# Preparing six of eight tiles inside the scan steps, and outer products written to PSUM in pairs of words

## The reference, cut to what matters

```
xn    = layernorm(x)
bc    = xn @ W_bc.T                          # 64 + 32 + 32 columns
delta = softplus(bc[..., :64] @ W_dt.T + b_dt)
B, C  = bc[..., 64:96], bc[..., 96:128]
h     = exp(delta * A) * h + (delta * xn) * B      # for each step of time, channel, state
y     = sum over the states of h * C  +  xn * D_param
x     = x + y
```

## Time and profile before

| | |
|---|---|
| median of three runs | 1005.86 us |
| profiled execution, its own time | 1001.59 us |
| its span, first to last instruction | 999.9 us |
| first scan starts | 222.79 us |
| last scan ends | 812.71 us |
| PE busy | 873.0 us, 87% |
| DVE busy | 831.2 us, 83% |
| ACT busy | 460.2 us, 46% |
| POOL busy | 395.3 us, 40% |
| DMA engines busy, mean | 38.1% of the span |
| mean granted TensorE clock | 0.903 |

### The profile page before, as it was taken

The page is one execution under the profiler, slowest core; times in us unless marked ns, Lnnn a source line. Parts: engine busy times, 40 slices in busy tenths (PEclk is TensorE's granted clock), DMA queues, the critical chain, the costliest instruction groups (busy, mean ns, idle before and its releaser), DMA issues.

```text
span 999.9 us, 22490 instructions
## 1 busy us (share of the span) xinstructions
PE 873.0 (87%) x7440; PEld 670.1 (67%) x7440; DVE 831.2 (83%) x861; ACT 460.2 (46%) x798; POOL 395.3 (40%) x737
## 2 busy tenths in 40 slices
PE   5666666159999999999999999999999969899994
PEld 3434444148777777777777777777777747787873
DVE  6655765307999999999999999999999976899884
ACT  1554444533454545544545545454545334443631
POOL 6253333412333333333333333333333544456434
PEclk9776555556999999999999999999999989999997
DMA  9399999392222222222222221222222334210101
GB/s 329 84 150 162 165 170 171 88 163 82 64 65 78 61 76 67 59 77 66 61 79 63 68 72 61 76 64 61 79 64 64 110 106 138 56 51 22 43 22 63
DMA packets 206072, 89.93 MB, mean 90 GB/s; under 512 B 139220, under 2 KB 191956, under 8 KB 205268
## 3 DMA queue, kind: packets, MB, share of 16 engines
q1 hardware_dynamic: 206036, 89.49, 38.1%
HBM read 45.85 MB, written 43.61 MB: 89 GB/s over the span
## 4 chain that ended last, share of the span: by engine, by line
PE 65%; SPq 16%; DVE 8%; POOL 4%; issue 3%; ACT 2%; DMA 1%; ACTq 0%; DVEq 0%; POOLq 0%
PE psum L1329 23%; PE psum L1298 13%; PE psum L1286 11%; PE psum L1336 9%; SPq L974 7%; SPq L1027 6%; PE psum L458 5%; POOL arena L399 2%; DVE arena L1606 2%; SPq L991 1%; POOL arena L390 1%; SPq L968 1%; PE psum L527 1%; DVE delta_mov L706 1%; ACT arena L564 1%
## 5 line engine op out<-in xcount | busy, mean ns | idle before, releaser
L1606 DVE TENSOR_TENSOR_SCAN arena<-arena,psum 128x1024 f32<-128x1024 f32 x256 | 570.9, 2274 | 48.4 <-DMA delta_terms<-arena 29.4
L1429 ACT ACTIVATE arena<-psum 128x512 f32<-128x512 f32 x512 | 278.0, 595 | 303.4 <-PE psum L1286 299.7
L1329 PEld LDWEIGHTS psum<-du_mov,b_sta 96*128 96x128 bf16 x2048 | 206.8, 131 | 130.2 <-DVE arena L1606 127.2
L1329 PE MATMUL psum<-du_mov,b_sta 96*128 96x128 bf16 x2048 | 273.0, 315 | 13.2 <-DVE arena L1606 13.1
L1180 POOL TENSOR_TENSOR carry<-arena 128x64 f32<-128x64 f32 x252 | 110.7, 439 | 357.0 <-DVE arena L1606 270.4
L1286 PE MATMUL psum<-delta_mov,a_sta 96*128 96x128 bf16 x2048 | 163.5, 224 | 8.3 <-ACT arena L1429 8.3
L1286 PEld LDWEIGHTS psum<-delta_mov,a_sta 96*128 96x128 bf16 x2048 | 144.1, 110 | 11.2 <-ACT arena L1429 10.7
L1336 PE MATMUL psum<-carry,ident 128*128 128x32 f32 x1024 | 149.2, 270 | 0.0
L1336 PEld LDWEIGHTS psum<-carry,ident 128*128 128x128 f32 x1024 | 148.4, 206 | 0.0
L1298 PE MATMUL psum<-arena,c_sta 128*32 128x512 f32 x1024 | 148.0, 643 | 0.0
L458 PE MATMUL psum<-delta_mov,arena 128*128 128x256 f32 (+6 forms) x544 | 114.6, 368 | 8.0 <-ACT arena L579 7.9
(11 more groups left out here) (142 smaller groups left out, 819.7 us busy)
## 6 DMA issues: line engine op xcount, KB each, us to landing
du_terms<-arena SPq DMA_DIRECT2D x48, 256.0 KB, 3.9
du_mov<-du_terms SPq DMA_DIRECT2D x128, 96.0 KB
y<-y_rows SPq DMA_DIRECT2D x32, 256.0 KB
b_terms<-delta_mov SPq DMA_DIRECT2D x6, 1024.0 KB, 10.6
delta_terms<-arena SPq DMA_DIRECT2D x48, 128.0 KB, 5.3
delta_mov<-delta_terms SPq DMA_DIRECT2D x128, 48.0 KB
b_sta<-b_terms SPq DMA_DIRECT2D x64, 96.0 KB
arena<-in_L_attn_x SPq DMA_DIRECT2D x8, 512.0 KB, 5.3
```

Source lines behind the costliest of these rows:

```text
L1329: mm = nc.tensor.matmul(sub(psum, 0, P, o, (4, 4), (TS, GD // 2)), b_sta[k][0:ROWS, (s * 4 + tg) * P:(s * 4 + tg + 1) * P], sub(du_mov[k], ...
L1429: nc.scalar.activation(sub(arena, 0, P, k * CHUNK_ELEMS + u * 16 * TS, (TS, 16), (D * TS, SUBS), (1, TS)), sub(psum, 0, P, (4 + u % 2) * B ...
L1606: nc.vector.tensor_tensor_scan(state[s][:, seg], decay[k][:, (s * D + g * GD) * TS:(s * D + (g + 1) * GD) * TS], psum[:, 2 * (step % 2) * ...
```

## The change

*Preparation.* Only tiles 0 and 1 are prepared ahead of the scans. Tiles 2 to 7 are prepared within the 32 scan steps of a tile, two tiles ahead: while tile lt is scanned, tile lt + 2 is prepared (EARLY = 2). Each engine's list gets pieces (`p_piece`) behind the work of a step, by the number n of the step in the tile, 0 to 31:

- SP: x at the tile's start, behind a wait for all stores of the tile before; base in the second chunk, b in the third, delta and du in the fourth, the delta stores ahead of the y store, the du stores behind it, and the loads for the chunk after the next behind that.
- VectorE: statistics at 2 and the shift -mean * rstd at 4, nothing else.
- ACT: the normalisation at 5 (four activations of 256), copies of transposes at 6 and 7, Abs and Relu of the pre-activation at 11 and 15, Exp and the copies of c and b at 16, b at 17 and 18 with Ln at 18, delta's high part at 22, du at 23 and 24 with delta's middle part, du's high part at 26 and middle part at 28 (two casts of 1024 each).
- POOL: rstd at 3, base at 6 and 8, b's parts at 18 and 19, delta at 20, du at 21, delta's rest at 23 and low part at 25, du's rest at 27 and low part at 29.
- TensorE: transposes of xn at 6 and 7, the products for delta one a step at 8 to 15, c and b at 16, transposes of b at 17 and of du at 23 and 24.

Delta is now made with channels on the partitions, from xn transposed and one product of the two weights, W_dt W_bc (`w_eff`), made once. It needs no transpose; du does.

*Buffers.* The decay of a chunk's first half has one buffer in place of two, so the exponentials of the next chunk start two steps later and wait group by group for the scan (AHEAD = 2). y has one row buffer and one bank in place of two. Bank 7 is used for the preparation.

*Outer products.* The scratch rows of du hold, for each channel, a zero word-half and the value (512 bf16 in place of 256), in three parts and not six terms. The operand is loaded so that two time steps stand interleaved, the first row block with its value in the even place and the second in the odd one. A matmul still has 96 rows and 128 columns, and its output is pairs of adjacent words, two pairs at a distance of 8, in place of single words at a distance of 4. The loads for a chunk are 12 DMAs of du, 4 of b and 12 of delta. The delta scratch is laid out by tile, so that parts and batches have one stride.

*Zero fill.* The fill of the b scratch is issued by ACT, in three DMAs, and no longer by SP in six.

The core of the diff:

```
-                            for half in range(2):
-                                for tg in (1, 2, 3, 0):
-                                    o = (pair_bank + half) * BANK + tg
-                                        sub(psum, 0, P, o, (4, 4), (TS, GD // 2)),
-                                        sub(du_mov[k], 0, ROWS, (s * 4 + tg) * D + d0, (DU_COLS, 4), (1, GD // 2)),
+                                    o = (pair_bank + half) * BANK + 4 * tg
+                                        sub(psum, 0, P, o, (2, 2), (TS, GD // 2), (1, 2)),
+                                        sub(du_mov[k], 0, ROWS, (s * 4 + tg) * DU_ROW + 2 * d0, (DU_SIDE, 2), (1, GD)),

 # SP, within the scans
+            def m_tile(lt, first, stream, last):
+                p = lt + EARLY
+                if stream:
+                    sp_.wait_ge(terms_stored[0], 16 * STORES * (p - 1))
+                    load_x(p, 0)
+                for kk in range(CT):
+                    c, k = CT * lt + kk, kk % 2
+                    if not (last and kk >= 2):
+                        sp_.wait_ge(S["args_ready"], (c + 1) * UNITS)
+                        ...
+                        load_md(lt + (kk + 2) // CT, (kk + 2) % CT)
+                    if stream and kk == 1:
+                        store_base(p, 0)
+                    if stream and kk == 3:
+                        sp_.wait_ge(S["dlo_ready"], p)
+                        store_delta(p, 0)
+                    if not (first and kk == 0):
+                        store_y(c - 1)
+                    if stream and kk == 2:
+                        store_b(p, 0)
+                    if stream and kk == 3:
+                        sp_.wait_ge(S["ulo_ready"], p)
+                        store_du(p, 0)
+                    if not (last and kk >= 2):
+                        sp_.wait_ge(S["b_ready"], (c + 1) * STEPS)
+                        load_mu(c + 2, k)

 # POOL, behind the carry and the reset of step n
+            def p_piece(p, n, first):
+                if n == 3:
+                    rstds(p, 0)
+                if n == 6:
+                    pool.wait_ge(S["xn_ready"], p - 1)
+                    base_product(p, 0, sp[0])
+                if n == 8:
+                    base_sum(p, 0, sp[0])
+                ...
+                if n == 20:
+                    delta_sum(p, 0)
+                if n == 21:
+                    du_product(p, 0)
+                if n == 23:
+                    delta_rest(p, 0)
+                if n == 25:
+                    delta_low(p, 0)
+                if n == 27:
+                    du_rest(p, 0)
+                if n == 29:
+                    du_low(p, 0)

 # VectorE, behind the scan of step n
+            def p_piece(p, n, first):
+                if n == 2:
+                    dve.wait_ge(x_loaded[0], 16 * p)
+                    statistics(p, 0)
+                if n == 4:
+                    dve.wait_ge(S["rstd_ready"], p + 1)
+                    nc.vector.scalar_tensor_tensor(out=shift, in0=mv[0][:, 0:7:2], scalar=-1.0, in1=rstd[0], ...)

 # ACT, behind the exponentials of step n
+                if n == 18:
+                    b_middle(p, 0)
+                    ln_part(p, 0)
+                if n == 22:
+                    act.wait_ge(base_stored[0], 16 * p)
+                    delta_high(p, 0)
+                if n == 24:
+                    take_du(p, 0, 1, 7)
+                    delta_middle(p, 0)
+                if n == 26:
+                    du_high(p, 0)
+                if n == 28:
+                    du_middle(p, 0)
```

More of the change, by code:

```diff
@@ L1165, in m_pair @@
                             G = c * STEPS + s * GROUPS + g
[L1166 removed]
+                            early = start and s == 0
                             if s == 0:
@@ L1321, in m_pair @@
                             pair_bank = 2 * (step % 2)
-                            if not (first and k == 0 and step < 2):
+                            if not (start and step < 2):
                                 pe.wait_ge(S["scan_done"], G - 1)
```

1056 lines of the change are left out of this document (586 added, 470 removed).

## The result

| | before | after |
|---|---|---|
| median | 1004.1 us (999.96 to 1007.05, 4 runs) | 1050.0 us (1044.0 to 1055.6, 4 runs) |
| ratio after / before | | 1.046, 95% interval 1.039 to 1.053 |
| profiled execution, its span | 999.9 us | 1050.3 us |
| scan 4 starts | 234.35 us | 112.06 us |
| last scan ends | 812.7 us | 860.0 us |

The change makes the kernel 4.6% slower; 972 us, faster, was forecast. Scan 4 does start 122 us earlier, but the six tiles that prepare another one take 98 to 111 us each. Executions of one kernel differ here by up to 5%, with the mean granted clock; the disturbed ones are left out of all ratios, and for e5 and e11, which had only one undisturbed each, the text gives the median of all and the spread.

What follows compares the result with a forecast made beforehand. TensorE was taken as the bound by 0.1 us a step, VectorE right behind. 110 + 549.4 + 8 + 13 + 59 + 12 + 27 = 778.4 us to the last scan's end; with tail 187.2, span 966, median 972; range 885 to 1020.

Steps and rivals of the forecast that it cites:

- Preparation before the scans: SP's queue before the scans: with two tiles to store, scan 4 starts at 110 us (100 to 130); gain 124.
- the pairs: Outer products on TensorE: writing pairs of words takes eight from 0.87-0.98 to 0.5 us, so VectorE sets 2.18 a step.
- Rival 3: Outer products: pairs gain nothing, TensorE stays the bound at 2.28 us a step; median 1032 us, slower; chance 0.09.
- VectorE's own work: Statistics, aggregates and shift of a streamed tile on VectorE, hidden by nothing: 2.2 us a tile, 13 us for six.
- rival 2: SP becomes the bound if a load issues at 0.74 us instead of 0.45; median 1085 us, slower; chance 0.07.
- POOL's order: POOL's pieces wait for ACT's and stand ahead of the carry, stalling scans: 9.8 us a tile, 59 us for six.
- Together 5 x 5.5 = 27 us: SP's order at the tile's end: wait for x 2.8 us plus slow clock 2.7, in five tiles.
- Together 2 us: ACT's and TensorE's added work in a streamed tile: 2 us a tile (0 to 5), 12 us for six.
- The granted clock: TensorE at half clock after VectorE's pause of some 5 us at the statistics: 2.7 us a tile (0 to 15).
- leaves 0.3: ACT at step 18: two table loads and other work exceed free time by 2.8 us; TensorE's buffers leave 0.3 unhidden.
- The wait for x: VectorE waits for x, issued behind stores and 16 operand loads: 2.8 us (0 to 12) in five tiles, none in the first.
- The condition for being wrong: Wrong if chunks without preparation stay at 18.3 us, SP shows no idle time, or streamed tiles take under 76 or over 100.

Runs made afterwards that it cites:

- e5: Kernel after with x of the next tile issued ahead of the operand loads, loop kept over tiles 1 to 4; 1022 us (1005 to 1028).
- e11: e9 with Ln of the streamed tiles replaced by a further Exp, so no table change; 978 us (949 to 998).
- e14: e9 with one table set, statistics and later pieces earlier, two delta parts stored a chunk earlier, x of tile 2 before the scans; ratio 0.937 to the kernel before.
- e1: Kernel before with only the outer products' writes changed to pairs of adjacent words; ratio 0.976 to the kernel before, 24 us less.
- e6: Kernel after with the outer products writing single words at a distance of 4 again, operand kept; 1071 us, ratio 1.066 to the kernel before.
- e3: Kernel after with the loop written out and x of the next tile issued ahead of the operand loads; 1015 us, ratio 1.012 to the kernel before.
- e7: e3 with preparation pieces at other steps, ACT's mostly three steps ahead of the POOL pieces waiting for them; 1012 us, ratio 1.008 to the kernel before.
- e16: Kernel after with VectorE writing a buffer of its own behind the fifth scan of tiles 6 and 7, as a pause; ratio 1.068 to the kernel before.
- e9: e7 with a separate buffer for x, issued in the third chunk of the tile before; 1006 us, ratio 1.002 to the kernel before.
- e8: e3 with the outer products made three times at six steps of each streamed tile, as filler; 993 us, ratio 0.992 to the kernel before.
- e2: Kernel after with the loop over tiles 1 to 5 written out, nothing else changed; ratio 1.042 to the kernel before.
- e13: Kernel after with one table set for both exponential and logarithm loaded ahead of the scans, Ln kept; ratio 1.027 to the kernel before.
- e15: e14 with the outer products made three times at step 2 of each streamed tile, as filler; 934 us, ratio 0.934 to the kernel before.
- e17: e16 with TensorE repeating the seventh step's outer products, 5 times in tile 6 and 13 in tile 7; ratio 1.066 to the kernel before.

## Why the prediction was wrong

*Right.* Preparation before the scans: scan 4 at 110 forecast, 112.06 measured. It is half luck. What held it was x of tile 2 (15.81 us), which the text took to be early in the first tile. SP issued that x behind the same stores (100.06 us), so it came when they did: in e14, with x issued early, the scans wait for du's stores to land, and scan 4 starts at 107.57. The pace of 2.178 us; the pairs, which e1 and e6 price at 24 and 20 us. The first eight outer products at full clock show 0.62 us busy and are followed 0.45 us later. Rival 3, and the rule of the Trainium skill, "PSUM — Partial Sum Buffer", Specifications, taken strictly, fall with it: pairs of words are a broken pattern and run here as quickly as a row, and the measurement decides. It fits the lines of 8 bytes of that section; that they are the reason is not shown. VectorE's own work was 2.2 us. SP's loads: the 112 of tile 3 of the kernel after average 0.45 us, as forecast, so rival 2 did not come. The tail, 190.3 for 187.2.

*POOL's order.* Forecast 9.8 us a tile. Steps 23 to 30 lie 10.3 above pace, and moving the pieces took away 10.1 of them (e3 to e7), of which 2.6 came back at 10 to 22. In the kernel after POOL waits 4.8, 3.5, 3.1 and 3.6 us for ACT's pieces there. The mechanism was right. The size was short: the four pieces of these steps are 5.1 of the 7.0 us summed, so some 7 of the 9.8, and steps 6 and 7 add 1.8 us where the clock is up (e3, tile 4) and 4.2 where it is down.

*The step that failed* is "Together 5 x 5.5 = 27 us" in the part on SP, and beside it "Together 2 us" in the part on ACT and TensorE. With 5.5 us a tile it had the wait for x, and the clock behind it; one mechanism was missing, and three terms were too small.

1. The granted clock, which I put at 2.7 us a tile behind one pause. The earlier trace rows showed 0.50 behind an idle stretch, and I read it as a price of up to 1 us on some steps. But at 0.50 two steps cost TensorE 7.0 us, so TensorE becomes the bound. The slow steps cost 10 us behind a pause of 2.3 us of VectorE (e16) and 21 behind 6.6 (e9), and 2.5 behind one of 5.0 (e7). Tile 3 of the kernel after has four pauses of TensorE over 1.5 us: 3.28 for a carry behind the statistics, 2.04 at the tables, 1.68 for a carry behind a cast, 6.25 at the jump. What the clock costs there in all no run tells: filling pauses at six steps of a tile, each in part, gained some 20 us on e3 (e8).
2. The jump back, absent from the prediction. 8.7 to 9.0 us for 2.18 at four seams, 3.9 and 4.0 at the loop's entry and exit: 30 us in all. Taken away alone it gave nothing (e2), since the wait for x stood behind it. The kernel before has a loop too, over 16 steps where the new one has 32, with 18 transfers of q8 in all and no such pause to read it from.
3. The table loads: "leaves 0.3". ACT's excess of 2.8 us was in the text; what was wrong is that two units of buffer and a lead of 1 us would hide 2.5 of it. With the clock up, steps 18 to 22 lay 1.9 above pace (tile 0), and the fallen clock made that 4.7; e13 took 3.7 of it away.
4. The wait for x, 2.8 us forecast in five tiles and nothing in the first. It was 15.8 in the first. It is 7.1 in tile 1 and 1.1 or less in the others, because there the jump stands in front; without the jump it is 4.5 to 9.1 (e2, step 2 at 8.6 to 13.2 less 4.1). The landing was too short: 4.6 us in the text, from a queue without stores in it, and 8.1 at the seam of e2 shown above; and from the start of du's stores to the first load behind them it was 4.0 us, for 2.5.

For a tile with the wait for x the forecast had 19.5 us above pace (2.2 + 9.8 + 2 + 5.5), and the ledger has 35.4, a mean of tiles 1 to 5: 10.3 from POOL at 23 to 30, 6.6 at 4 to 9 (POOL and clock), 4.7 tables, 2.0 TensorE's products, 6.0 statistics and x, 5.7 the seam. Five times the difference is 80 of the 82 us by which the last scan ended late (860.0 for 778.4). The condition for being wrong, tiles over 100 us, was met.

*What stays open.* Why instructions are loaded anew at some jumps and not at others. What sets the length of a stretch at low clock. How the 6.6 us at steps 4 to 9 divide between POOL's order and the clock. Whether operand loads two chunks ahead can be made safe at 2.18 us a step: the versions with the stalls out met them late (e9, e14, e15).

## What to carry to other kernels

A wait has two prices: its length, and what it does to TensorE's clock. Where TensorE at 1.2 GHz would be the bound, the second can be the larger: a pause of 2.3 us cost 12.2 us in all in e16, though one of 5.0 only 7.5 in e7. So look for short pauses in an engine with slack, and if one can't be removed, give TensorE work in it that changes nothing, such as the same product into the same place. And stalls cover each other: of the changes that removed one known stall here (e2, e7) the time did not move until the next in line (x, then the operands) was removed too. A ledger of step lengths shows such a move where the total shows nothing. Last, before interleaving a function with exponentials, load the table set that has both.

## What the runs showed of the hardware

- Matmul output in pairs of adjacent 4-byte words: eight of 128 columns in 0.45 us from start to start, as in a row; single words at a distance of four, 0.84 (831.43 to 832.27 in e6).
- At 14 of 30 jumps back over a body of 32 steps TensorE, with no semaphore outstanding, stood 3.4 to 7.1 us, and two 16 KB transfers of the instruction queue q8 ran there. At the other 16 it stood 0.4 at most and q8 had none. A lap behind a pause cost some 9 such transfers (69 in all in after, 42 in e13).
- The granted clock went from 1.00 to 0.50 behind a pause of TensorE of 1.98 us (tables), of 2.62 (e16) and of 3.23 (e17, tile 7), and not behind one of 0.84 (e17, tile 6) or behind the 1.98 us of the tables in tile 0 of the kernel after. It stayed at 0.50 for 10.2 us (e7 and e15, tile 6), 27.3 (e16, tile 6) and 61.4 (e9, tile 6).
- One activation table set serves Exp and Ln; loaded once, it saves 2 x 1.28 us at each change.
